# Moving a token permutation off VectorE's write side: GpSimd's sums in runs of four, ScalarE's copies with a step of 16 bytes

## The chip, the cores and the metric

One core of one Trainium2 chip. The metric is the device time of one execution in microseconds. Of the kernel before there are three timed runs and one profiled execution.

## The reference

A two-layer transformer on 2,048 tokens (2 sequences of 1,024) with 256 features. Layer 0 is causal attention with 32 query heads and 8 key/value heads of size 8, beside a gelu feed-forward in fp8. Layer 1 has an attention of a different kind, and a ternary-weight feed-forward. The change touches layer 1's attention alone. What is computed there is this:

```
def apply_rope(x, inv_freq):
    angle = t * inv_freq[None, :]
    x1, x2 = (x[..., ::2], x[..., 1::2])
    return jnp.concatenate([x1 * cos - x2 * sin, x1 * sin + x2 * cos], axis=-1)
q = (x @ wq.T).reshape(b, s, H, HD)      # H = 16 heads of HD = 16
k = (x @ wk.T).reshape(b, s, H, HD)
v = (x @ wv.T).reshape(b, s, H, HD)
q = apply_rope(q, inv_freq)
k = apply_rope(k, inv_freq)
scores = jnp.einsum('bshd,bstd->bsht', q, k) / jnp.sqrt(jnp.float32(HD))
weights = jax.nn.softmax(scores, axis=-1)
attn = jnp.einsum('bsht,bstd->bshd', weights, v)
```

So every token attends over its own 16 heads: one 16x16 table of scores for each token, none between tokens.

## The kernel before, in words

The 2,048 tokens are 16 tiles of 128. Each engine runs one fixed list of steps, written out by hand in the table ORDER (one list for TensorE, ScalarE, VectorE, GpSimd, and SyncE, which issues most DMAs). A step waits on semaphores for its inputs and for the buffers that it overwrites, so whatever stands behind a waiting step on the same engine waits too. Layer 0's attention runs through nearly all of the program in 144 "quads": four score matmuls (step qk, L761) into the four banks of psS, two exponentials of 1,024 columns on ScalarE (exp, L1057), and eight matmuls with the values (pv, L775). The score matmuls of the next quad need the banks that the exponentials of this one have read. All other work is fitted between the quads.

Layer 1's score path of tile n goes through these steps:

- **qkv1** (TensorE, L853): projected queries and keys, transposed, land in one PSUM bank as 512 columns: 2 halves (even and odd dimensions), times query and key, times 128 tokens. Three PSUM banks (psA, psB, psC) are handed round between all steps of this sort, in program order.
- **rab** (VectorE, L1512): two multiplications by cosine and sine tables from that bank into r1. A token t of the tile is a*16 + c, with a from 0 to 7 and c from 0 to 15. The output pattern puts the tokens in the order (c, a), so the 16 values that follow each other in time are written 8 floats, 32 bytes, apart. When both are done the bank is free.
- **rr** (GpSimd, L1799): a subtraction and an addition of halves of r1 into rqkv, 256 columns each, all three operands contiguous. Its outcome is 8 blocks of 32 tokens, in the order query/key, then block b = c div 4.
- **rw** and **rd** (SyncE, L563 and L571): 2 DMAs write the blocks to the DRAM scratch rscr, 4 DMAs read them back into qk1T, one for each block b: there the 16 dimensions of a head lie on the partitions, and heads and the block's 32 tokens along the columns.
- **kq** (ScalarE, L1122): two copies, queries and keys, of 512 columns from qk1T into qk1Tg (the trace calls it kTf), which bring together the tokens of one group j = c mod 4. The input pattern has runs of 8 floats. The rows of qk1T also hold an indicator pattern (ind2, read once by step mk), which masks scores between different tokens.
- **S1** (TensorE, L914): 16 matmuls from those groups into psS; then ex1 (ScalarE, L1131), PV1 (TensorE, L925), o1r and o1 (VectorE, L1552 and L1562), and a round trip through the scratch o2scr to `at`.

The pattern that reads qk1T, the products and the sums are these lines of the kernel before:

```
return qk1T[:, s, :, :].rearrange("p j n -> p (j n)").rearrange("p (h j a) -> p j h a", j=4, a=8)
...
e.tensor_tensor(r1[:, k, :].rearrange("p (e s c a) -> p e s a c", e=2, s=2, a=8), bank,
                table.unsqueeze(2).to_broadcast([128, 2, 2, 8, 16]), ALU.mult)
...
e.tensor_tensor(dst[:, 256 * f:256 * f + 256], r1[:, f, 0:256], r1[:, f, 256:512], op)
```

Of the kernel before, what the change touches and what calls it, by code (L numbers as in the profile page):

```python
# [6 lines left out]
ALU = mybir.AluOpType  # L7
ACT = mybir.ActivationFunctionType
AX = mybir.AxisListType
F32 = mybir.dt.float32  # L10
# [7 lines left out]
NT = 16  # L18
# [223 lines left out]
def shared_banks():  # L242

    fills = [s for s in first_pass("pe") + second_pass("pe") if s[0] in EMPTIED]
    return {s: k for k, s in enumerate(fills)}, fills
# [30 lines left out]
def flat(a):  # L276
    return a.rearrange("p a n -> p (a n)")


def build(nc, A):  # L280
    ctx = ExitStack()
    with ctx:
        def sb(name, shape, dt=F32):
            return ctx.enter_context(nc.sbuf_tensor(name, shape, dt))
# [4 lines left out]
        def ps(name):  # L289
            return ctx.enter_context(nc.psum_tensor(name, [128, 512], F32))  # L290

        S = {n: ctx.enter_context(nc.semaphore("s_" + n)) for n in SEMS}
# [2 lines left out]
        psV = ps("psV")  # L295
        psM = [ps("ps" + c) for c in "ABC"]
        qkvscr = nc.dram_tensor("qkvscr", [NT, 3, 128, 256], F32, kind="Internal").ap()
        rscr = nc.dram_tensor("rscr", [NT, 2, 4, 16, 512], F32, kind="Internal").ap()
        vscr = nc.dram_tensor("vscr", [NT, 16, 128, 16], F32, kind="Internal").ap()
        o2scr = nc.dram_tensor("o2scr", [NT, 16, 128, 16], F32, kind="Internal").ap()  # L300
        oscr = nc.dram_tensor("oscr", [NT, 128, 256], F32, kind="Internal").ap()
# [21 lines left out]
        turns = big[:, 1024:4096].rearrange("p (e n) -> p e n", e=3)  # L323
# [56 lines left out]
        r1 = sb("r1", [128, 2, 512])  # L380
# [3 lines left out]
        qk1T = sb("qk1T", [128, 2, 4, 128])  # L384
        G3vodd = flat(w8l[:]).bitcast(F32)[:, 512:1024].rearrange("p (g d) -> p g d", d=32)
        qk1Tg = flat(kTf[:])[:, 1280:2304].rearrange("p (s j n) -> p s j n", s=2, n=128)
# [31 lines left out]
            return (qk1Tg if n < NT else qk1T)[:, s, :, :]  # L418

        def landed(s):  # L420
            return qk1T[:, s, :, :].rearrange("p j n -> p (j n)").rearrange("p (h j a) -> p j h a", j=4, a=8)

        def of_group(n, s, b, j):

# [8 lines left out]
        def read_groups(n):  # L433

            return 64 * (n // 2 + 1) + (0 if n % 2 else 128)

        tst = [flat(r1[:]), qk1T[:].rearrange("p s j n -> p (s j n)")]
        filled, fills = shared_banks()
# [41 lines left out]
        def sp(e):  # L480
# [76 lines left out]

            def rw(n):
                src = flat(rqkv[n % 2][:, 0:2, :]).rearrange("p (f m t) -> p f m t", f=2, t=32)
                dst = rscr[n].rearrange("s b (f i) (h t) -> f (i h) (s b) t", f=2, t=32)  # L560
                for f in range(2):
                    w.wait_ge("rr", 2 * n + f + 1)
                    e.dma_start(dst[f], src[:, f, :, :]).then_inc(S[f"d_rw{n % 2}"], 16)  # L563

            def rd(n):
                w.wait_ge(f"d_rw{n % 2}", 32 * (n // 2 + 1))
                w.wait_ge("d_rd0", 128)
                w.wait_ge("kq", KQ * n)
                for b in range(4):
                    dst = qk1T[32 * b:32 * b + 16, :, :, :].rearrange("p s j n -> p s (j n)")  # L570
                    e.dma_start(dst, rscr[n, :, b].rearrange("s d n -> d s n")).then_inc(S[f"d_rd{n % 2}"], 16)  # L571

            def ow(n):
                w.wait_ge("o1", 2 * n + 2)
# [52 lines left out]
            def all_landed(passes):  # L627
# [8 lines left out]
                w.wait_ge("d_ht", 16 * NT * passes)  # L636

            run = {"first": first, "lc": lc, "lw": lw, "mk": mk, "rw": rw, "rd": rd, "wg": wg, "wt": wt, "vw": vw, "vr": vr, "ow": ow, "at1r": at1r, "out": out, "kt": kt, "qt": qt, "xt": xt, "ht": ht}
            ahead = e.mark_branch_hint_location()
            for name, n in first_pass("sp"):  # L640
# [357 lines left out]
        def act(e):  # L998
# [119 lines left out]
            def kq(n):  # L1118
                w.wait_ge(f"d_rd{n % 2}", read_groups(n))
                w.wait_ge("S1", 4 * n)  # L1120
                for s in range(2):
                    e.activation(qk1Tg[:, s, :, :].rearrange("p j (h a) -> p j h a", a=8), landed(s), ACT.Copy).then_inc(S["kq"], 1)  # L1122

            def ex1(n):
                w.wait_ge("w8", 6)
# [24 lines left out]
            def hxa(n):  # L1150
                w.wait_ge("rsg", n + 1)
                e.activation(hx_b[:, 0, :], h1, ACT.Copy, scale=ss[n % len(ss)][:, 2:3]).then_inc(S["hxa"], 1)  # L1152

            run = {"tTc": tTc, "wgx": wgx, "lx": lx, "wh": wh, "wsq": wsq, "qh": qh, "g": g, "hxa": hxa, "sin": sin, "tc": tc, "tde": tde, "exp": exp, "sq": sq, "fh": fh, "th": th, "qk1c": qk1c, "kq": kq, "gTk": gTk, "ex1": ex1,
                   "tg": tg, "ssq": ssq}
            load_small()
# [15 lines left out]
        def dve(e):  # L1172
# [328 lines left out]
                                ALU.mult).then_inc(S["v1c"], 1)  # L1501

            def rab(n):
                bank = psM[filled["qkv1", 2 * n] % len(psM)][:].rearrange("p (e s a c) -> p e s a c", e=2, s=2, a=8)
                t0 = 128 * (n % NB)
                w.wait_ge("tTc", 5)
                w.wait_ge("tc", 12)
                w.wait_ge("qkv1", 2 * n + 1)
                w.wait_ge("rr", 2 * n)
                for k in range(2):  # L1510
                    table = turns[:, k:k + 2, t0:t0 + 128].rearrange("p e (a c) -> p e a c", a=8)
                    e.tensor_tensor(r1[:, k, :].rearrange("p (e s c a) -> p e s a c", e=2, s=2, a=8), bank,  # L1512
                                    table.unsqueeze(2).to_broadcast([128, 2, 2, 8, 16]), ALU.mult).then_inc(S["rab"], 1)

            def ro1(n):
                cb = cos1[:, n % NB, :].unsqueeze(1).unsqueeze(1).to_broadcast([128, 2, 16, 8])
# [132 lines left out]
            def fl(n):  # L1649
# [7 lines left out]
                   "tw": tw, "ln0": ln0, "xn": xn, "xnTc": xnTc, "qkvc": qkvc, "va": va, "wide": wide, "q0": q0, "kl": kl, "xs": xs,  # L1657
                   "fTc": fTc, "rmax": rmax, "mTc": mTc, "ob": ob, "att": att, "attTc": attTc, "xa": xa, 
                   "ge1": ge1, "ge3": ge3, "yff": yff, "ln1": ln1, "xn1": xn1, "xn1Tc": xn1Tc, "v1c": v1c, "rab": rab, "ro1": ro1,
                   "ro2": ro2, "gTq": gTq, "m1": m1, "gTm": gTm, "o1r": o1r, "o1": o1, "sg": sg, "hh": hh,  # L1660
                   "ssm": ssm, "hx": hx, "at1Tc": at1Tc, "yo": yo, "yout": yout}
# [15 lines left out]
        def pool(e):  # L1677
# [116 lines left out]
            def rr(n):  # L1794
                dst = flat(rqkv[n % 2][:, 0:2, :])
                w.wait_ge("rab", 2 * n + 2)
                w.wait_ge(f"d_rw{n % 2}", 32 * (n // 2))
                for f, op in enumerate((ALU.subtract, ALU.add)):
                    e.tensor_tensor(dst[:, 256 * f:256 * f + 256], r1[:, f, 0:256], r1[:, f, 256:512], op).then_inc(S["rr"], 1)  # L1799

            def rsg(n):
                sn = ss[n % len(ss)]
# [2 lines left out]
                e.tensor_tensor(sn[:, 2:3], sn[:, 1:2], mhalf[:], ALU.pow).then_inc(S["rsg"], 1)  # L1805

            run = {"zero": zero, "gz": gz, "gz2": gz2, "rr": rr, "zf": zf, "w8a": w8a, "rs0": rs0, "rope": rope, "ql": ql, "mask": mask,
                   "ge4": ge4, "xf": xf, "rs1": rs1, "ro1p": ro1p, "rsg": rsg}
            ahead = e.mark_branch_hint_location()
# [35 lines left out]
def consts():  # L1845

    p = np.arange(128)
    ident = np.eye(128, dtype=np.float32)
    f = (1.0 / np.float32(10000.0) ** (np.arange(0, 8, 2, dtype=np.float32) / np.float32(8))).astype(np.float32)
    ang = (np.arange(1024, dtype=np.float32)[:, None] * f[None, :]).astype(np.float32)  # L1850
    c = np.repeat(np.cos(ang), 2, axis=1).astype(np.float32).reshape(8, 128, 8).transpose(1, 0, 2)
    s = np.repeat(np.sin(ang), 2, axis=1).astype(np.float32).reshape(8, 128, 8).transpose(1, 0, 2).copy()
    s[:, :, 0::2] *= -1
    mneg = np.where(p[None, :] > p[:, None], np.float32(NEG), np.float32(0))
    pos = (np.arange(8)[None, :] * 128 + p[:, None]).astype(np.float32)
    same = (np.arange(512)[None, :] % 8 == np.arange(8)[:, None]).astype(np.float32)
    ind2 = np.stack([NEG * same, 1.0 - same]).astype(np.float32)
    one = (p[:, None] // 16 == np.arange(8)[None, :]).astype(np.float32)
    ind1 = np.stack([NEG * one, 1.0 - one], axis=1).astype(np.float32)
    return {"ident": ident, "cs0": np.ascontiguousarray(c) * np.float32(UP), "sn0": np.ascontiguousarray(s) * np.float32(UP), "mneg": mneg, "pos": pos,  # L1860
            "ind1": ind1, "ind2": ind2}
# [35 lines left out]
```

## Time and profile before

| | us |
|---|---|
| median of 3 runs (lowest to highest) | 557.74 (557.38 to 558.65) |
| the profiled execution | 560.62 |
| span of its trace | 558.9 |
| TensorE busy in the span | 520.7 |
| ScalarE busy | 471.9 |
| VectorE busy | 381.5 |
| GpSimd busy | 233.8 |

The profiled execution took 1.7 us beside its span, and 2.9 us more than the median of the timed runs. Busy time of TensorE is modelled from its pipelined matmuls, so a short wait inside a merged group of them can be counted as busy. A row of the timeline gives start and length in us, then engine, line, operation, tiles and shape. "x2" or "x4" in it is the number of instructions merged into one row, and a bracket at the end of a row gives the idle time of the engine before it and what ended it.

### The profile page before, as it was taken

To read this page: it belongs to the slowest core of one execution; us is meant where nothing else is said; L and a number is where in the kernel's file an instruction comes from. 1 tells how busy PE (TensorE), PEld (TensorE's weight loads), DVE (VectorE), ACT (ScalarE), POOL (GpSimd) and SP (SyncE) were. 2 spreads that over 40 slices of the span, in tenths; PEclk is the share of its full clock that TensorE was granted. 3 is DMA by queue.
4 is the path that set the end of the run, shared out by engine and by line. 5 is a ranking of instruction groups with operands and counts; after the bars stand their busy time and mean duration, and the time that the engine had idled before them with its cause. 6 is when DMAs were issued, how large, how long until landed. Compare 5 with 4: busy or idle time off the path is not lost.

```text
span 558.9 us, 12847 instructions
## 1 busy us (share of the span) xinstructions
PE 520.7 (93%) x4872; PEld 261.7 (47%) x4920; DVE 381.5 (68%) x794; ACT 471.9 (84%) x614; POOL 233.8 (42%) x299
## 2 busy tenths in 40 slices
PE   7678999999999999999999999999999999998875
PEld 3323335434354555545555455564455353556544
DVE  5838887788779767766676787656554544756755
ACT  0579999999999999999989989988898998974440
POOL 3556745726534246344664565133082220160200
PEclk8869999999999999999999999999999999999988
DMA  7932112112443622345306454564533318347863
GB/s 246 326 84 58 26 41 57 41 33 39 76 82 47 103 47 59 53 66 79 67 12 122 62 83 67 93 99 67 110 56 66 64 40 142 67 83 130 112 112 88
DMA packets 211344, 46.18 MB, mean 83 GB/s; under 512 B 198544, under 2 KB 207888, under 8 KB 211280
## 3 DMA queue, kind: packets, MB, share of 16 engines
q1 hardware_dynamic: 208832, 42.37, 41.0%
q10 hardware_dynamic: 2448, 2.95, 1.7%
q8 instruction: 40, 0.66, 0.5%
q14 instruction: 24, 0.20, 0.1%
HBM read 19.09 MB, written 10.49 MB: 53 GB/s over the span
## 4 chain that ended last, share of the span: by engine, by line
PE 68%; ACT 13%; DVE 7%; DMA 5%; issue 4%; SPq 1%; POOL 1%; ACTq 0%; DVEq 0%
PE psV L775 20%; PE psS L761 8%; ACT Pt L1057 6%; PE psC L961 3%; PE psS L914 3%; PE psA L961 2%; PE psC L971 2%; PE psB L961 2%; DMA at<-o2scr 2%; DVE r L1512 2%; DMA stage<-in_wg 2%; PE psC L853 2%; PE psB L971 2%; PE psB L812 1%; PE psA L853 1%
## 5 line engine op out<-in xcount | busy, mean ns | idle before, releaser
L1057 ACT ACTIVATE Pt<-psS 128x1024 f32<-128x1024 f32 x288 | 279.9, 1031 | 27.2 <-PE psS L761 22.6
L775 PE MATMUL psV<-Pt,vaug 128*32 128x512 f32 x1152 | 150.6, 606 | 1.3 <-POOL Pt L1753 0.9
L1753 POOL TENSOR_SCALAR_AFFINE_SELECT Pt<-Pt 128x1024 f32<-128x1024 f32 x64 | 71.9, 1148 | 70.9 <-ACT Pt L1057 70.9
L761 PE MATMUL psS<-qTf,kTf 32*128 32x512 f16 x576 | 69.0, 388 | 7.7 <-DMA kTf<-QXf 4.2
L761 PEld LDWEIGHTS psS<-qTf,kTf 32*128 32x128 f16 x576 | 18.6, 91 | 92.3 <-ACT Pt L1057 47.0
L1805 POOL TENSOR_TENSOR ss<-ss,mhalf 128x1 f32<-128x1 f32 x16 | 9.3, 582 | 92.5 <-DVE ss L1589 92.5
L775 PEld LDWEIGHTS psV<-Pt,vaug 128*32 128x32 f32 x1152 | 25.0, 108 | 39.9 <-issue 31.1
L1131 ACT ACTIVATE stage<-psS 128x1024 f32<-128x1024 f32 x32 | 31.0, 1021 | 8.9 <-PE psS L914 8.8
L1799 POOL TENSOR_TENSOR rqkv<-r 128x256 f32<-128x256 f32 x32 | 24.9, 800 | 30.0 <-DVE r L1512 30.0
L1733 POOL TENSOR_TENSOR rt<-qkv,cs 128x320 f32<-128x320 f32 x16 | 15.1, 942 | 44.5 <-DVE QXf L1334 35.1
L1744 POOL TENSOR_TENSOR QXf<-rt,QXf 128x512 f16<-128x512 f32 x16 | 21.2, 1327 | 28.9 <-ACT QXf L1044 28.9
L1427 DVE SCALAR_TENSOR_TENSOR ga<-gw,gb 128x512 bf16<-128x512 f32 x32 | 23.1, 722 | 6.1 <-ACT gw L1083 6.1
L1418 DVE SCALAR_TENSOR_TENSOR gw<-gw,gb 128x512 f32<-128x512 f32 x32 | 25.1, 783 | 2.3 <-ACT gw L1072 2.2
L961 PE MATMUL psC<-wguT,xhs 128*128 128x512 bf16 x90 | 23.7, 380 | 2.4 <-issue 1.7
L1595 DVE SCALAR_TENSOR_TENSOR qtmp<-qtmp,ss 128x1024 f16<-128x1024 f32 x16 | 22.5, 1408 | 3.2 <-ACT qtmp L1152 3.2
L1152 ACT ACTIVATE qtmp<-qtmp,ss 128x1024 f16<-128x1024 f32 x16 | 18.5, 1158 | 4.5 <-POOL ss L1805 4.4
L1736 POOL TENSOR_TENSOR rt<-qkv,sn 128x160 f32<-128x160 f32 x32 | 21.9, 706 | 0.0
L1072 ACT ACTIVATE gw<-gb 128x512 f32<-128x512 bf16 x32 | 20.9, 653 | 0.0
L1083 ACT ACTIVATE gw<-gw 128x512 f32<-128x512 f32 x32 | 20.7, 646 | 0.0
L1512 DVE TENSOR_TENSOR r<-psC,big 128x512 f32<-128x512 f32 x14 | 14.5, 1120 | 8.9 <-PE psC L853 8.9
L1147 ACT ACTIVATE qtmp<-qtmp 128x1024 bf16<-128x1024 f32 x16 | 17.0, 1060 | 3.9 <-DVE qtmp L1583 2.4
L914 PE MATMUL psS<-kTf 24*128 24x128 f32 x512 | 19.5, 283 | 0.0
(339 smaller groups left out, 1088.1 us busy)
## 6 DMA issues: line engine op xcount, KB each, us to landing
rscr<-rqkv SPq DMA_DIRECT2D x32, 128.0 KB, 2.8
qk1T<-rscr SPq DMA_DIRECT2D x64, 64.0 KB, 3.0
vscr<-rqkv SPq DMA_DIRECT2D x16, 128.0 KB, 3.3
o2scr<-o SPq DMA_DIRECT2D x16, 128.0 KB, 1.7
at<-o2scr SPq DMA_DIRECT2D x16, 128.0 KB, 3.3
out<-yout SPq DMA_DIRECT2D x16, 128.0 KB, 2.7
x<-in_x ACTq DMA_DIRECT2D x3, 512.0 KB, 5.5
stage<-in_wg SPq DMA_DIRECT2D x2, 512.0 KB, 9.8
```

Of the source, the lines that this page charges most:

```text
L761: e.matmul(psS[j], kd[32 * j:32 * j + k, h, 128 * at:128 * at + 128], qd[32 * j:32 * j + k, 4 * h:4 * h + 4, :].rearrange("p s n -> p (s n ...
L775: ins = e.matmul(psV[32 * j:32 * j + 32, :], vaug[:, at, j, 32 * h:32 * h + 32], Pt[(4 * Q + j) % NP], start=(kb == 0 and h == 0), stop=(k ...
L914: ins = e.matmul(psS[b][:, 128 * j:128 * j + 128], of_group(n, 1, b, j), of_group(n, 0, b, j), start=True, stop=True)
L961: ins = e.matmul(bank[:], src[:, pt, 128 * c:128 * c + 128], wguT[:, c, c0:c0 + 512], start=(k == 0), stop=(k == 3))
L1057: e.activation(flat(Pt4[:, u % NP:u % NP + 2, :]), flat(psS4[:, j:j + 2, :]), ACT.Exp, scale=scale).then_inc(S["exp"], 1)
L1131: e.activation(P1[:, 4 * b:4 * b + 8, :].rearrange("p g n -> p (g n)"), flat(psS4[:, b:b + 2, :]), ACT.Exp, scale=SC1).then_inc(S["ex1"], 1)
L1418: e.scalar_tensor_tensor(gw[:, half, :], gw[:, half, :], 1.0 / GA, gb[:, half, :], ALU.add, ALU.mult).then_inc(S["ge1"], 1)
L1427: e.scalar_tensor_tensor(a, gw[:, half, :], 1.0, gg, ALU.add, ALU.mult).then_inc(S["ge3"], 1)
L1512: e.tensor_tensor(r1[:, k, :].rearrange("p (e s c a) -> p e s a c", e=2, s=2, a=8), bank, table.unsqueeze(2).to_broadcast([128, 2, 2, 8, 1 ...
L1595: e.scalar_tensor_tensor(hx_b[:, 1, :], h1, sn[:, 2:3], hx_b[:, 0, :], ALU.mult, ALU.subtract).then_inc(S["hx"], 1)
L1753: e.affine_select(out=p, in_=p, pattern=[[0, 8], [1, 128]], compare_op=ALU.is_ge, fill=0.0, base=0, channel_multiplier=-1).then_inc(S["mas ...
L1799: e.tensor_tensor(dst[:, 256 * f:256 * f + 256], r1[:, f, 0:256], r1[:, f, 256:512], op).then_inc(S["rr"], 1)
```

## The change

The tokens of a tile reach the scores in the same groups as before; what changes is who permutes them.

- VectorE's two products (rab) write r1 in the order in which they read, with consecutive columns.
- GpSimd's two sums (rr) read r1 in runs of four tokens, c mod 4, with 16 tokens between one run and the next, and write consecutive columns. Block b = c div 4 now stands ahead of query/key in rqkv.
- The scratch rscr has its dimensions for query/key and block exchanged. The number, the size and the rows of the DMAs rw and rd stay: 128 x 8 x 32 elements in each of 2 writes, 16 x 2 x 512 in each of 4 reads.
- ScalarE's copies (kq) read every fourth float, 16 bytes apart, in place of runs of 8; they write as before.
- The indicator ind2, a constant of the host, follows the new order of columns.

No instruction is added, removed or moved on any engine.

```
-        rscr = nc.dram_tensor("rscr", [NT, 2, 4, 16, 512], F32, kind="Internal").ap()
+        rscr = nc.dram_tensor("rscr", [NT, 4, 2, 16, 512], F32, kind="Internal").ap()
...
-            return qk1T[:, s, :, :].rearrange("p j n -> p (j n)").rearrange("p (h j a) -> p j h a", j=4, a=8)
+            return qk1T[:, s, :, :].rearrange("p j n -> p (j n)").rearrange("p (m j) -> p j m", j=4)
+
+        def by_run(a):
+            return a.rearrange("p (m b j) -> p b m j", b=4, j=4)
...
-                dst = rscr[n].rearrange("s b (f i) (h t) -> f (i h) (s b) t", f=2, t=32)
+                dst = rscr[n].rearrange("b s (f i) (h t) -> f (i h) (b s) t", f=2, t=32)
...
-                    e.dma_start(dst, rscr[n, :, b].rearrange("s d n -> d s n")).then_inc(S[f"d_rd{n % 2}"], 16)
+                    e.dma_start(dst, rscr[n, b].rearrange("s d n -> d s n")).then_inc(S[f"d_rd{n % 2}"], 16)
...
-                    e.activation(qk1Tg[:, s, :, :].rearrange("p j (h a) -> p j h a", a=8), landed(s), ACT.Copy).then_inc(S["kq"], 1)
+                    e.activation(qk1Tg[:, s, :, :], landed(s), ACT.Copy).then_inc(S["kq"], 1)
...
-                bank = psM[filled["qkv1", 2 * n] % len(psM)][:].rearrange("p (e s a c) -> p e s a c", e=2, s=2, a=8)
+                bank = psM[filled["qkv1", 2 * n] % len(psM)][:].rearrange("p (e s t) -> p e s t", e=2, s=2)
...
-                    table = turns[:, k:k + 2, t0:t0 + 128].rearrange("p e (a c) -> p e a c", a=8)
-                    e.tensor_tensor(r1[:, k, :].rearrange("p (e s c a) -> p e s a c", e=2, s=2, a=8), bank,
-                                    table.unsqueeze(2).to_broadcast([128, 2, 2, 8, 16]), ALU.mult).then_inc(S["rab"], 1)
+                    e.tensor_tensor(r1[:, k, :].rearrange("p (e s t) -> p e s t", e=2, s=2), bank,
+                                    turns[:, k:k + 2, t0:t0 + 128].unsqueeze(2).to_broadcast([128, 2, 2, 128]),
+                                    ALU.mult).then_inc(S["rab"], 1)
...
-                    e.tensor_tensor(dst[:, 256 * f:256 * f + 256], r1[:, f, 0:256], r1[:, f, 256:512], op).then_inc(S["rr"], 1)
+                    e.tensor_tensor(dst[:, 256 * f:256 * f + 256].rearrange("p (b m j) -> p b m j", b=4, j=4),
+                                    by_run(r1[:, f, 0:256]), by_run(r1[:, f, 256:512]), op).then_inc(S["rr"], 1)
...
-    same = (np.arange(512)[None, :] % 8 == np.arange(8)[:, None]).astype(np.float32)
+    same = (np.arange(512)[None, :] // 4 % 8 == np.arange(8)[:, None]).astype(np.float32)
```

## Rows read from the trace of the kernel before

**Rows 1.** Page parts 1 and 4: busy time by engine; the chain of waits by line
```profile
PE 520.7 (93%) x4872; PEld 261.7 (47%) x4920; DVE 381.5 (68%) x794; ACT 471.9 (84%) x614; POOL 233.8 (42%) x299
...
PE psV L775 20%; PE psS L761 8%; ACT Pt L1057 6%; PE psC L961 3%; PE psS L914 3%; PE psA L961 2%; PE psC L971 2%; PE psB L961 2%; DMA at<-o2scr 2%; DVE r L1512 2%; DMA stage<-in_wg 2%; PE psC L853 2%; PE psB L971 2%; PE psB L812 1%; PE psA L853 1%
```

**Rows 2.** Stages: us; PE, PEld, DVE, ACT, POOL busy; TensorE clock; DMA share, GB/s
```profile
130.00:200.00 70.00, 67.69 (x676) 33.45 (x676) 55.29 (x111) 67.37 (x91) 29.52 (x42) 1.00 0.44 75
200.00:300.00 100.00, 99.10 (x1002) 53.44 (x1006) 71.52 (x156) 94.56 (x128) 48.76 (x61) 1.00 0.35 62
300.00:400.00 100.00, 98.62 (x1020) 51.41 (x1027) 68.48 (x146) 91.11 (x118) 43.05 (x54) 1.00 0.52 82
400.00:495.00 95.00, 93.94 (x864) 43.37 (x868) 50.30 (x102) 85.66 (x105) 30.80 (x40) 1.00 0.40 71
495.00:559.00 64.00, 49.71 (x574) 34.64 (x577) 39.13 (x88) 26.12 (x37) 9.49 (x14) 0.95 0.66 110
```

**Rows 3.** VectorE's products (L1512) by bank: ns min/median/max, first and last start
```profile
L1512 DVE TENSOR_TENSOR r<-psC,big x14: 1093/1124/1152, 180.9 to 498.7; 128x512 f32<-128x512 f32 x14
L1512 DVE TENSOR_TENSOR r<-psA,big x12: 1078/1103/1159, 167.3 to 519.0; 128x512 f32<-128x512 f32 x12
```

**Rows 4.** Two VectorE operations with consecutive writes (L1574; L1399 with a broadcast input)
```profile
L1574 DVE SCALAR_TENSOR_TENSOR stmp<-stmp,psC x14: 671/687/690, 165.3 to 541.5; 128x512 f32<-128x512 f32 x14
...
L1399 DVE TENSOR_TENSOR att<-psA,rec x7: 424/424/425, 46.7 to 392.9; 128x256 f32<-128x256 f32 x7
```

**Rows 5.** Timeline of TensorE where it waited for L1512, between 130 and 495 us
```profile
140.78 0.91 PE L714 MATMUL psB<-wqkv,xnT 128*128 128x384 f32 x2 [0.58 <-DVE r L1512]
...
169.43 0.91 PE L714 MATMUL psA<-wqkv,xnT 128*128 128x384 f32 x2 [0.59 <-DVE r L1512]
...
333.27 0.81 PE L961 MATMUL psC<-wguT,xhs 128*128 128x512 bf16 x3 [0.31 <-DVE r L1512]
```

**Rows 6.** Timeline of the last two rotations: what stands around L1512
```profile
498.29 1.08 PE L925 MATMUL psB<-stage,w8l 128*32 128x128 f32 x32
499.66 0.68 DVE L1552 COPY o1r<-psB 128x512 f32<-128x512 f32 x1
...
520.16 0.83 PE L858 MATMUL psA<-wqkv,xhs 128*128 128x256 f16 x6 [0.68 <-DVE r L1512]
520.92 1.17 PE L914 MATMUL psS<-kTf 24*128 24x128 f32 x32
```

**Rows 7.** ScalarE's copies (L1122) and other SBUF-sourced ScalarE operations, by source line
```profile
L1122 ACT ACTIVATE kTf<-qk1T x32: 613/637/696, 153.4 to 535.7; 128x512 f32<-128x512 f32 x32
...
L1083 ACT ACTIVATE gw<-gw x32: 629/641/690, 32.3 to 479.3; 128x512 f32<-128x512 f32 x32
...
L1147 ACT ACTIVATE qtmp<-qtmp x16: 1057/1058/1070, 150.5 to 543.8; 128x1024 bf16<-128x1024 f32 x16
```

**Rows 8.** Timeline after the first pair of copies: ScalarE, then TensorE
```profile
153.40 1.15 ACT L1122 ACTIVATE kTf<-qk1T 128x512 f32<-128x512 f32 x2
...
160.52 1.94 ACT L1057 ACTIVATE Pt<-psS 128x1024 f32<-128x1024 f32 x2
...
160.06 0.39 PE L761 MATMUL psS<-qTf,kTf 32*128 32x512 f16 x4
...
162.22 0.68 PE L761 MATMUL psS<-qTf,kTf 32*128 32x512 f16 x4
```

**Rows 9.** Timeline: the third pair and TensorE after it; ScalarE after the twelfth
```profile
193.92 1.19 ACT L1122 ACTIVATE kTf<-qk1T 128x512 f32<-128x512 f32 x2
...
197.22 0.39 PE L761 MATMUL psS<-qTf,kTf 32*128 32x512 f16 x2 [0.18 <-ACT Pt L1057]
...
485.60 1.94 ACT L1057 ACTIVATE Pt<-psS 128x1024 f32<-128x1024 f32 x2 [1.00 <-PE psS L761]
```

**Rows 10.** GpSimd's sums (L1799), and a product in rows of four (L1736)
```profile
L1799 POOL TENSOR_TENSOR rqkv<-r x32: 722/731/1708, 135.4 to 520.9; 128x256 f32<-128x256 f32 x32
...
L1736 POOL TENSOR_TENSOR rt<-qkv,sn x32: 587/602/1587, 12.8 to 413.4; 128x160 f32<-128x160 f32 x32
```

## The prediction

> **What bounds the kernel now.** I read the page first, then the busy time by stage, then the three lines that the change touches, and last the timeline around them. The page says TensorE: it is busy for 93% of the span, and the chain of waits consists mostly of its matmuls [rows 1]. The stage table shows that a share over the whole span hides how close ScalarE is [rows 2]. Over the 365 us from 130 to 495, TensorE is busy for 67.69 + 99.10 + 98.62 + 93.94 = 359.4 us, which leaves 5.6 us idle, and ScalarE for 67.37 + 94.56 + 91.11 + 85.66 = 338.7 us, which leaves 26.3. VectorE is busy for 245.6 us of it and GpSimd for 152.1, so neither is short of time; their delays matter only where somebody waits. TensorE's granted clock is full there. From 495 on all engines have gaps, and the path runs through transfers and short steps.
>
> Between TensorE and ScalarE the coupling is tight: four score matmuls need banks that two exponentials must have read. When nothing holds them, four take 0.39 us; at 162.22 they took 0.68, since the second two could start only when the exponentials of the row at 160.52, ending at 162.46, were through [rows 8]. So "busy" contains short waits for ScalarE that no idle column shows. Most of what follows hangs on this.
>
> **VectorE's products get shorter.** There are 32 of them (2 in each of 16 tiles), and they take about 1.11 us [rows 3]. The nearest operation with the same 512 columns, PSUM as one input, SBUF as another and fp32 out, but consecutive writes, takes 0.687 [rows 4]. I take that: 1.11 - 0.69 = 0.42 us less for each, 0.84 for a pair, 13.5 us of VectorE time in all. The other end is no saving (if the broadcast table, which stays, is what costs); another product with a broadcast input, 256 columns in 0.424, speaks against that [rows 4]. Little of the 13.5 is on the path. The chain gives L1512 2% of the span, some 11 us [rows 1], but TensorE had other matmuls to run during most of it; what it can win is its idle time. Between 130 and 495 us it waited for these products at three places, 0.58, 0.59 and 0.31 us, each under what the products become shorter: 1.5 us [rows 5]. Of the last two tiles, the pair before the copy at 499.66 sits on the path, but that copy also needs the matmuls of 498.29, which end at 499.37, so 0.3 at most. At 520.16 TensorE waited 0.68, but the scores of tile 14 at 520.92 wait for ScalarE's copies, not for VectorE, so most of that turns into a longer wait there; I count 0.2 [rows 6]. Sum: **2.0 us gained**, with 1 and 3 as ends.
>
> **ScalarE's copies read with a step of 16 bytes.** 32 copies of 0.637 us each now read runs of 8 floats, and cost the same as a contiguous activation with SBUF input, 0.641 [rows 7]. So runs of 32 bytes cost nothing. No row shows ScalarE reading single elements far apart. Lower end: no cost. Upper end: the nearest row for single elements at a large step is VectorE's write with 32 bytes between elements, which costs 0.42 more for 512 elements than the consecutive one [rows 3, 4]. For ScalarE, 512 more elements cost 1.058 - 0.641 = 0.417 us, so one lost slot for each element comes to the same 0.42 [rows 7]. If each element took VectorE's whole 1.11 / 512 = 2.17 ns, a copy would take 1.11, or 0.47 more. I take 0.42, since VectorE's row is the only one here with one element per place fetched, and its extra is just that of one slot per element: a copy of **1.06 us**, a pair 0.84 us later.
>
> What 0.84 us costs at the end depends on ScalarE's next gap. I followed ScalarE from each of the 12 pairs before 495 us until either its gaps made up 0.84 us or a score matmul started as its exponential ended. The first pair, at 153.40, finds no gap before the contact at 162.22, so TensorE loses nearly all of it [rows 8]. The third, at 193.92, meets TensorE already waiting for it at 197.22. The twelfth has a gap of 1.00 before the row at 485.60, and only a contact ahead of that gap costs something [rows 9]. By this reading four pairs (tiles 0, 2, 3, 9) cost about 0.8 each, four (1, 6, 7, 8) about 0.55, two (4, 11) about 0.3 and two (5, 10) nothing: 3.2 + 2.2 + 0.6 = 6.0. Behind 495 the copies of tile 14 delay the scores at 520.92 [rows 6], 0.6 more. TensorE's 5.6 us of idle take back perhaps 1. Sum: **5.6 us lost**, with 0 and 8 as ends.
>
> Here a rule speaks against the change. The row: VectorE's writes with a single float per 32 bytes take 1.11 us where consecutive ones take 0.69 [rows 3, 4]. The Trainium skill, "SBUF — State Buffer", in the note on cachelines under "Door 1: The DMA port swizzle", says that SBUF has lines of 16 bytes and that full bandwidth needs two or more accesses to a line. A step of 16 bytes is one access to a line, so by that rule the copies slow down; by the row of the contiguous activation alone they would not, and the sum would be -2.0.
>
> **GpSimd's sums read in runs of four.** Two a tile, 0.731 us now [rows 10]. The nearest row with short runs is the rotation product of layer 0, 160 elements with a step of 8 bytes in rows of four: 0.602, or 3.8 ns an element. At that rate 256 take 0.96; the lower end is 0.73. I take 0.8, nearer to the contiguous end, since the elements inside a run stay neighbours. At the upper end a pair is 0.46 later, less than the 0.84 by which the products end sooner. The two DMAs behind it, the masks and the power steps queued behind it on GpSimd (busy for 152 of 365 us [rows 2]) are covered by that and by the time to the copies: the first sum starts at 135.4 and the first copy at 153.4, 18 us later [rows 7, 10]. Cost: 0. Without that cover it would be 16 x 0.14 = 2 us. Product, sum and copy are queued where they were, SyncE's DMAs keep number and size, so the exchanged dimensions of rscr cost 0: the transfer is hidden in the same 18 us.
>
> **The sum.** -2.0 + 5.6 + 0 = +3.6. Against the profiled execution, 560.6 us beside a span of 558.9, that is 564.2; that execution was 2.9 above the median of the timed runs, 557.74, which I forecast from: 557.7 + 3.6 = 561.3. My sum for ScalarE has more ways to come out smaller than larger (a contact moved past a gap costs nothing), so I round down to **560.9**.
>
> **The rivals.**
> *ScalarE doesn't mind the step.* Then only the products' gain is left: 557.7 - 2.0 = 555.7, with 554.5 to 556.8. For it: 32-byte runs are free, and ScalarE's 0.82 ns per element (0.417 / 512) leaves memory more slack than one element per VectorE slot may. Against: VectorE's row. It decides at 2.0 / 5.6 x 0.42 = 0.15: a copy that becomes longer by less than 0.15 us makes the change a gain. The same note of the Trainium skill also says that four fp32 is as far as one can stride for free, which speaks for this case; no row here shows a step of exactly 16 bytes.
> *The products don't get shorter*, since the broadcast table or the two tables in one instruction cost the time: 0 gained, 5.6 lost, 563.3; without ScalarE's cost 557.7, no change, so the change wouldn't do what it says. Against: the product with a broadcast input and consecutive writes, whose 0.424 us for 256 columns fits 0.687 for 512 [rows 4].
> *GpSimd becomes slow.* If each run of four is handled as a row of its own and a sum takes 1.5 us, a pair is 1.5 later, 0.7 more than the products give back; masks and the reciprocal roots behind it come late in some tiles, and I put 8 x 0.3 = 2.4 us on it: 558.1 with free copies. The Trainium skill, "GPSIMD Engine Reference", section "Performance pitfalls for Q7 kernels", says that reads with a step above 8 bytes cost half as much again; inside a run of four the step is 4 bytes, and at half as much again (1.1 us) the pair would be covered.
>
> **How the numbers follow.** Three runs of the kernel before spread over 1.3 us, so I take 0.2%, 1.1 us, as what a measurement can tell from no change. The forecast case has 0.56: within it slower 0.46, same 0.08, faster 0.02. The free step has 0.36: faster 0.27, same 0.08, slower 0.01. Unchanged products have 0.05: slower 0.03, same 0.02. Slow GpSimd has 0.03, 0.01 each. Sum: faster 0.30, same 0.19, slower 0.51. The likeliest case's own range is 558.5 to 563.8. The range over all cases goes from 554.6, near the low end of the free step, to 563.8; a tenth is left out on either side.
>
> **What the changed profile would show.** The products near 690 ns. The copies near 1,060 ns (forecast) or 640 (first rival), and that row settles the sign. The sums at 730 to 960 ns. ScalarE's busy time up by 32 x 0.42 = 13 us, VectorE's down by as much. TensorE's waits for L1512 gone between 130 and 495, and more or longer waits of the score matmuls for L1057. I am wrong if the copies stay at 640, or if they double and the time stays: then ScalarE's gaps had taken the delay in.

## The result and the profile after

| | before | changed |
|---|---|---|
| median of 4 runs, us | 557.98 (557.38 to 558.65) | 570.78 (568.65 to 574.83) |
| the profiled execution, us | 560.62 | 568.65 |
| span of its trace, us | 558.9 | 566.9 |

The ratio is 1.0242, with a 95% interval from 1.0202 to 1.0281: 13 us slower. The forecast had the sign right and the likeliest case right, but said 3.2 us and a range that ended at 563.8. In a second comparison with more runs, told below, the same kernel came to 1.0178 (1.0147 to 1.0208), 10 us. Both lie outside the range.

The three lines of the change, by source line (ns min/median/max, first and last start), in the changed kernel. They answer to [rows 3], [rows 7] and [rows 10]:

```profile
L1514 DVE TENSOR_TENSOR r<-psC,big x14: 678/685/693, 179.0 to 505.6; 128x512 f32<-128x512 f32 x14
...
L1125 ACT ACTIVATE kTf<-qk1T x32: 1113/1144/1255, 151.4 to 545.9; 128x512 f32<-128x512 f32 x32
...
L1802 POOL TENSOR_TENSOR rqkv<-r x32: 714/724/1803, 133.4 to 527.0; 128x256 f32<-128x256 f32 x32
```

The products are at 0.685 us, as taken. GpSimd's sums in runs of four cost what contiguous ones cost, 0.724. The copies went from 0.637 to 1.144, 0.51 us more each, 16 us for the 32. The page's busy line, and the stages (us; PE, PEld, DVE, ACT, POOL busy; clock; DMA share, GB/s), against [rows 1, 2]:

```profile
PE 527.7 (93%) x4920; PEld 262.9 (46%) x4920; DVE 370.6 (65%) x794; ACT 487.6 (86%) x614; POOL 232.0 (41%) x299
```

```profile
130.00:200.00 70.00, 68.32 (x671) 33.67 (x668) 50.80 (x108) 69.02 (x90) 30.41 (x42) 1.00 0.44 75
200.00:300.00 100.00, 98.63 (x997) 52.27 (x994) 68.74 (x152) 94.58 (x125) 47.70 (x59) 1.00 0.32 58
300.00:400.00 100.00, 98.04 (x1006) 52.26 (x1006) 64.81 (x145) 92.72 (x115) 41.76 (x54) 1.00 0.48 76
400.00:495.00 95.00, 93.73 (x852) 42.29 (x848) 46.53 (x101) 87.18 (x102) 26.41 (x35) 1.00 0.43 78
```

ScalarE's busy time grew by 15.7 us. VectorE's fell by 10.9, less than the 13 that the prediction named: the products' own busy time fell by 12.5, and other lines of VectorE differ between the two traces by up to 0.9 either way. TensorE's share hardly moved: it is still "busy" for 358.7 of the 365 us. Whoever looks at busy shares alone sees a kernel bound by TensorE in both, and no reason for 8 us more span. The waits tell more. Here are TensorE's between 130 and 495 us in the changed kernel (engine, line waited for: us in total, times, longest); before, the first two lines of this list were 0 and 0.2 us, and L1512 stood in it with 1.5:

```profile
PE psS L917 <- ACT Pt L1060: 2.4, 8, 0.3
PE psS L764 <- ACT Pt L1060: 2.4, 5, 0.5
PE psC L856 <- ACT gb L1068: 0.6, 1, 0.6
PE psC L815 <- DVE stmp L1577: 0.5, 1, 0.5
```

The waits for the products are gone. The new first line is one that the prediction had not looked at: L917 (L914 before) is S1, the scores of layer 1 themselves, and it waits for the *exponentials* of layer 0, eight times.

### The profile page after: what moved, and what is told of

It reads as the page before. It is cut to its first block, busy times and chain, and to the rows that moved or that the text cites. A ratio compares the mean times of both kernels' runs of the same rounds, so it can differ in the third digit from the quotient of the medians.

```text
span 566.9 us, 12895 instructions
## 1 busy us (share of the span) xinstructions
PE 527.7 (93%) x4920; PEld 262.9 (46%) x4920; DVE 370.6 (65%) x794; ACT 487.6 (86%) x614; POOL 232.0 (41%) x299
## 4 chain that ended last, share of the span: by engine, by line
PE 58%; ACT 24%; issue 7%; DVE 4%; DMA 3%; SPq 2%; POOL 1%; ACTq 0%; DVEq 0%; POOLq 0%
PE psV L778 17%; ACT Pt L1060 13%; PE psS L764 7%; ACT kTf L1125 4%; PE psS L917 3%; PE psC L964 3%; PE psA L964 2%; DMA stage<-in_wg 2%; PE psB L964 2%; PE psC L856 2%; PE psB L974 1%; DMA kTf<-QXf 1%; PE psB L815 1%; PE psA L815 1%; POOL Pt L1756 1%
## 5 line engine op out<-in xcount | busy, mean ns | idle before, releaser
L1125 ACT ACTIVATE kTf<-qk1T 128x512 f32<-128x512 f32 x32 | 35.2, 1162 | 0.3 <-DMA qk1T<-rscr 0.3
L1736 POOL TENSOR_TENSOR rt<-qkv,cs 128x320 f32<-128x320 f32 x16 | 16.0, 1003 | 45.4 <-DVE QXf L1337 35.8
L1747 POOL TENSOR_TENSOR QXf<-rt,QXf 128x512 f16<-128x512 f32 x16 | 19.9, 1245 | 29.6 <-ACT QXf L1047 29.6
L917 PE MATMUL psS<-kTf 24*128 24x128 f32 x512 | 23.2, 295 | 6.0 <-ACT kTf L1125 3.5
L964 PE MATMUL psC<-wguT,xhs 128*128 128x512 bf16 x104 | 27.7, 390 | 0.0
L917 PEld LDWEIGHTS psS<-kTf 24*128 24x128 f32 x512 | 18.9, 194 | 12.3 <-ACT kTf L1125 4.9
L964 PE MATMUL psB<-wguT,xhs 128*128 128x512 bf16 x80 | 20.6, 380 | 0.0
```

Of the source, the lines that this page charges most:

```text
L917: ins = e.matmul(psS[b][:, 128 * j:128 * j + 128], of_group(n, 1, b, j), of_group(n, 0, b, j), start=True, stop=True)
L964: ins = e.matmul(bank[:], src[:, pt, 128 * c:128 * c + 128], wguT[:, c, c0:c0 + 512], start=(k == 0), stop=(k == 3))
L1125: e.activation(qk1Tg[:, s, :, :], landed(s), ACT.Copy).then_inc(S["kq"], 1)
```

## The experiments

Eleven runs were made; the ninth is the changed kernel once more. All ratios are against the kernel before on the same chip.

**1. GpSimd does the whole permutation.**

```
# products as changed (consecutive columns); copies, rw, rd, rscr, ind2 as before; in rr:
-  e.tensor_tensor(dst[:, 256*f:256*f+256], r1[:, f, 0:256], r1[:, f, 256:512], op)
+  e.tensor_tensor(dst[:, 256*f:256*f+256].rearrange("p (s c a) -> p s c a", s=2, a=8),
+                  by_token(r1[:, f, 0:256]), by_token(r1[:, f, 256:512]), op)
# by_token(a) = a.rearrange("p (s a c) -> p s c a", s=2, a=8)
```

> VectorE's consecutive writes kept; GpSimd's sums do the whole permutation (reads with a step of 64 bytes), so ScalarE's copies and the DMAs stay as in the kernel before. Theory A (all of the loss is ScalarE's longer copies): copies back at 0.64 us, products at 0.69, time 1 to 3 us below the kernel before (555 to 557), whatever the sums take as long as that is under 1.6 us. Theory B (the loss comes from the changed order of r1 or from the products' earlier end, not from ScalarE): still 5 us or more above the kernel before. If GpSimd pays for each single element, its sums go from 0.73 to 1.1 or more.

Measured: 0.9966 (0.9934 to 0.9999), 1.9 us faster. The sums rose to 1.098 us, the copies were back at 0.637:

```profile
L1802 POOL TENSOR_TENSOR rqkv<-r x32: 1061/1098/2177, 136.2 to 519.8; 128x256 f32<-128x256 f32 x32
...
L1125 ACT ACTIVATE kTf<-qk1T x32: 612/637/698, 154.3 to 534.7; 128x512 f32<-128x512 f32 x32
```

Theory A holds: with short copies the shorter products are a small gain, the size forecast (2.0), and GpSimd's 0.37 us more a sum is covered. It is also the only version with the right groups that came out ahead of both kernels, if by little: its interval ends at 0.9999.

**2. One more copy a tile**, no strided read:

```
 for s in range(2):
+    if s == 0:
+        w.wait_ge("more", n)
+        e.activation(more, landed(s), ACT.Copy).then_inc(S["more"], 1)   # 512 columns, read by nobody
     e.activation(qk1Tg[:, s, :, :]..., landed(s), ACT.Copy).then_inc(S["kq"], 1)
```

> The kernel before plus one more ScalarE copy of 512 columns a tile, with the old pattern, into columns that nobody reads: 16 x some 0.52 us of ScalarE time, 8.3 us, and no strided read. Theory A (a delay of ScalarE goes through nearly in full): 6 to 8.5 us slower, 564 to 566. Theory C (my forecast's share, 5.6 of 13.4, and something else behind the rest): 3.5 us slower, 561 to 562.

Measured: 1.0077 (1.0038 to 1.0115), 4.3 us for 7.5 us more of ScalarE's busy time. Nearer to theory C; with an interval from 2.1 to 6.4 us theory A's lower end is not excluded.

**3. The copies in quarters**, the same pattern and data:

```
-    e.activation(qk1Tg[:, s, :, :]..., landed(s), ACT.Copy).then_inc(S["kq"], 1)
+    for j in range(4):
+        ins = e.activation(qk1Tg[:, s, j, :]..., landed(s)[:, j, :, :], ACT.Copy)
+    ins.then_inc(S["kq"], 1)
```

> The kernel before with each of the 32 copies cut into 4 copies of 128 columns, the same pattern and data: ScalarE pays fixed costs only, some 0.3 to 0.5 us more per 512 columns. Whatever a tile's copies take more by the trace, d: theory A says the time grows by 0.8 to 1.0 x 16 x d; theory C says 0.42 x 16 x d.

Measured: 1.0086 (1.0052 to 1.012), 4.8 us for 7.7 us of busy time. A share of 0.6 again, between the two theories, and the interval of 2.9 to 6.7 us excludes neither. A plain, unstrided delay of ScalarE costs time; whether it explains 15 us was open.

**4. The cost of a step, by itself.** The kernel before, and behind its last step:

```
+ src = stepped(big[:, 1024:4096], k)      # 384 fp32 elements, k elements apart; or dst in Pt
+ ScalarE: e.activation(dst, src, ACT.Copy)
+ VectorE, GpSimd: e.tensor_tensor(dst, src, src, ALU.mult)
```

> The kernel before with measurements behind its last step: 384 fp32 elements read from SBUF with a step of 1, 2, 3, 4, 5 and 8 elements, then written with a step of 2, 4 and 8, two of each on ScalarE, VectorE (product of a tensor with itself) and GpSimd. If lines of 16 bytes need two accesses each, steps of 1 and 2 cost the same and 4, 5, 8 more, 3 between. For ScalarE a step of 4 should then add about 0.37 us (0.5 x 384 / 512). If the cost grows with distance, 8 costs more than 4. Its total time means nothing.

The timeline of ScalarE: reads with a step of 1, 2, 3, 4, 5 and 8 elements, then writes with a step of 2 and 4:

```profile
555.66 0.52 ACT L500 ACTIVATE Pt<-big 128x384 f32<-128x384 f32 x1 [9.71 <-DVE flag L1685]
...
557.34 0.54 ACT L500 ACTIVATE Pt<-big 128x384 f32<-128x384 f32 x1
557.92 0.71 ACT L500 ACTIVATE Pt<-big 128x384 f32<-128x384 f32 x1
559.40 0.88 ACT L500 ACTIVATE Pt<-big 128x384 f32<-128x384 f32 x1
561.22 0.88 ACT L500 ACTIVATE Pt<-big 128x384 f32<-128x384 f32 x1
563.05 0.89 ACT L500 ACTIVATE Pt<-big 128x384 f32<-128x384 f32 x1
...
565.46 0.54 ACT L500 ACTIVATE Pt<-big 128x384 f32<-128x384 f32 x1
566.04 0.88 ACT L500 ACTIVATE Pt<-big 128x384 f32<-128x384 f32 x1
```

VectorE, reads with a step of 1, 3 and 4; then GpSimd, reads with a step of 1 and 8:

```profile
570.29 0.56 DVE L502 TENSOR_TENSOR Pt<-big 128x384 f32<-128x384 f32 x1
...
572.06 0.66 DVE L502 TENSOR_TENSOR Pt<-big 128x384 f32<-128x384 f32 x1
573.46 0.83 DVE L502 TENSOR_TENSOR Pt<-big 128x384 f32<-128x384 f32 x1
...
583.53 0.83 POOL L502 TENSOR_TENSOR Pt<-big 128x384 f32<-128x384 f32 x1 [38.76 <-DVE Pt L502]
...
589.03 0.88 POOL L502 TENSOR_TENSOR Pt<-big 128x384 f32<-128x384 f32 x1
```

On ScalarE and VectorE a step of 8 bytes costs next to nothing (0.54 and 0.56 us against 0.52 and 0.56), and 16 bytes the whole penalty (0.88 and 0.83); beyond 16 next to nothing is added. A step of 12 bytes costs half of the penalty on ScalarE (0.71) and over a third on VectorE (0.66). Writes behave as reads. The Trainium skill, "SBUF — State Buffer", in the note on cachelines under "Door 1: The DMA port swizzle", says that a line has 16 bytes and wants at least two accesses for full bandwidth. The trace agrees: on ScalarE 0.54 at a step of 2 elements, 0.88 at 4. The same note says that four fp32 is as far as one can stride for free. There the trace differs: step 4 is at 0.88, and the measurement decides. GpSimd loses 0.05 us of 0.83 in this form.

**5. The step alone**, in the kernel before. The groups of the scores then hold other tokens than they should:

```
-  landed: .rearrange("p (h j a) -> p j h a", j=4, a=8)
+  landed: .rearrange("p (m j) -> p j m", j=4)
```

> The kernel before with one pattern changed: ScalarE's copies read every fourth column. The groups of the scores then hold other tokens than they should; every instruction, DMA and size is that of before. Theory A (the copies' 0.5 us each is all of the loss): the changed kernel's loss plus what the first experiment gained, 12.8 + 1.9 = 14.7, so 570 to 574. Theory C (the delay costs 0.5 to 0.6 of itself, as in the two dose runs, and the rest of the loss comes from GpSimd's reads, rscr or the products): 16.2 x 0.55 = 9, so 566 to 568.

Measured: 1.0212 (1.0162 to 1.0262), 11.8 us slower: this one pattern costs about as much as the whole change. The loss lies between the theories' 14.7 and 9 us, with an interval (9.1 to 14.6) that reaches close to both; the next run decides.

**6. The changed kernel with copies of consecutive columns.** Here too the groups hold other tokens:

```
-  e.activation(qk1Tg[:, s, :, :], landed(s), ACT.Copy)
+  e.activation(qk1Tg[:, s, :, :], qk1T[:, s, :, :], ACT.Copy)
```

> The changed kernel with ScalarE's copies reading 512 consecutive columns; the groups of the scores then hold other tokens than they should, all else is as changed. Theory A: as the first experiment, 1 to 3 us under the kernel before. Theory C: 3 to 5 us over it.

Measured: 0.9952 (0.9922 to 0.9983), 2.7 us *faster* than before. Theory C falls: with the changed products, sums, scratch layout and DMAs in place, nothing of the loss is left once the copies are short (their median is 0.635 us here).

**7. Both doses at once** (2 and 3 together):

> The kernel before with both doses at once: one more copy of 512 columns a tile, and all copies cut in four; no strided read. ScalarE's extra time by the single doses is 7.5 + 7.7 = 15.2 us, nearly the changed kernel's 15.7 to 16.2. If a delay's cost grows in proportion (single doses: 4.3 and 4.8 us), it takes 9 us more, 567 to 568. If the first 0.5 us of a tile's delay finds slack that the second no longer finds, 12 to 15 us more, 570 to 574, and theory A holds with a cost that bends upwards.

Measured: 1.0200 (1.0154 to 1.0245), 11.2 us for 16.3 us more of ScalarE's busy time, beside 11.8 for 15.9 in run 5. Two plain kinds of delay cost what the step costs, so the step acts through time alone. The traces say it more sharply. From the first pair of copies to the twelfth, ScalarE takes 328.2 us before (153.40 to 481.58), 337.7 in run 5 and 337.8 here. Single doses sum to 9.1 us in the timed runs, less than the 11.2 of both, but within the noise. In the same stretch of the traces they add 3.9 and 4.1 us singly and 9.7 together, so the cost does bend upwards, though less than I had put.

**8. The copies on VectorE**, on top of run 1:

```
 ORDER["act"]: the 16 kq steps taken out;  ORDER["dve"]: put in at the places that correspond in time
-  e.activation(qk1Tg..., landed(s), ACT.Copy)
+  e.tensor_copy(qk1Tg..., landed(s))
```

> The first experiment's kernel (VectorE writes consecutive columns, GpSimd permutes all) with the copies of runs of 8 moved from ScalarE to VectorE, in VectorE's order at the places that correspond in time to ScalarE's in the first experiment. ScalarE's list loses 18.6 us of work, VectorE's gains 32 x about 0.6. Theory A, turned round (a tile's ScalarE time that goes away comes back at the end by half or more, until TensorE alone binds): 3 to 8 us under the first experiment, 548 to 553. If TensorE is the bound and ScalarE only when it is made slower: within 1.5 us of the first experiment, 554 to 557.

A miss: 1.0033 (1.0004 to 1.0062), 1.8 us slower than before and 3.7 slower than run 1, though ScalarE's busy time fell from 471.7 to 456.4 us. Most copies took 0.42 us there, some 1.3:

```profile
L1425 DVE COPY kTf<-qk1T x32: 404/420/1306, 151.1 to 536.7; 128x512 f32<-128x512 f32 x32
```

Time taken off ScalarE did not come back at the end. Between 130 and 495 us ScalarE now waits longer for TensorE's score matmuls, first in run 1, then here:

```profile
ACT Pt L1060 <- PE psS L764: 16.8, 36, 1.2
...
ACT Pt L936 <- PE psS L640: 25.2, 50, 1.2
```

So what mostly passes on when it is added gave nothing when it was taken away. The run is no pure subtraction: VectorE took the copies on, and in that stretch TensorE waits 1.8 us for VectorE, where run 1 has no such wait. What the shorter ScalarE list would give alone is not shown.

**9. The changed kernel once more**, five runs:

> The changed kernel once more, beside the next two and in more rounds, since its runs spread over 1.1%. By the traces the loss between 130 and 495 us adds up (9.5 for the copies, 1.7 back for the products), so I expect 2.12% less 0.34 to 0.48%, that is 1.65 to 1.8%, or 567 to 569 against 558; if it is 2.4% again, some 3 us more come from something that neither single change has.

Measured: 1.0178 (1.0147 to 1.0208), within the expected 1.65 to 1.8%. Copies (+2.12) and products (-0.34) add up; no third cost is needed. The first four runs had 1.0242, and the two intervals overlap by little. The two profiled executions, 566.9 and 570.2 us long, show where such spread comes from. From the first pair of copies to the twelfth they take 337.0 and 336.9 us. The 3.3 us between them lie ahead of 130 us (1.1 us, at a granted clock of 0.97 and 0.93) and behind the start of the last two exponentials (2.2 us, at 0.94 and 0.90).

**10 and 11. Values before scores.** In TensorE's order, `S1.n pv.m` became `pv.m S1.n` at eight tiles, in the changed kernel and in run 1's.

> The changed kernel with one more edit: in TensorE's order the scores S1 of tiles 0, 1, 4, 5, 7, 8, 9 and 10 go behind the quad's values matmuls (pv) that now follow them. S1 needs banks that two exponentials queued behind the long copies must have read; pv needs only older exponentials. Theory S (the contact that passes the copies' delay on is S1, not the next quad's score matmuls): TensorE no longer idles ahead of L917 for L1060 (8 places before, 2 to 4 now) and wins some 0.5 to 0.8 us at each of 6 to 8 tiles: 3 to 6 us under the changed kernel. Theory Q (the delay passes on at the next quad's score matmuls whatever S1 does), and also if ScalarE's ex1, which now comes later, costs what TensorE wins: within 1.5 us of the changed kernel, or slower.

> The first experiment's kernel with the same eight exchanges. With short copies S1 starts as its banks come free, so there is little idle time to win: theory S says 0 to 1.5 us under the first experiment (554 to 556), or up to 2 over it where ex1 comes later. If it wins as much as the run above, the exchange helps by itself and says nothing about the copies.

Measured: 1.0243 (1.0208 to 1.0277) and 1.0091 (1.006 to 1.0121). Both expectations missed. By the ratios both are slower than without the exchange, by 3.6 us (against run 9; the changed kernel's first four runs had 1.0242, no less than here) and 7.0. The exchange moved the wait instead of removing it: ScalarE's ex1 comes later, and now the next quad's score matmuls (L640 in this numbering) wait for *it*, in run 11:

```profile
PE psS L640 <- ACT stage L1010: 4.9, 13, 0.5
PE psS L640 <- ACT Pt L936: 0.2, 1, 0.2
```

Run 10 has the same first row with 4.8 us. ScalarE's own idle time ahead of ex1 grew as well, between 130 and 495 us from 1.9 (run 9) to 6.7 us in run 10, and from 2.8 (run 1) to 10.6 in run 11.

With the exchange the long copies cost 2.43 - 0.91 = 1.5%, without it 1.78 + 0.34 = 2.1%. The difference of 0.6% has an uncertainty of as much (four ratios, each known to 0.3 to 0.35%), and the longer gaps ahead of ex1 could take in a part of the delay by themselves. So these two runs don't show how much of the copies' cost runs through S1's place. The choice of tiles was not right for it either. In the changed kernel's trace S1 waits for an exponential at tiles 0, 1, 4, 6, 7 and 10. Tile 6, whose S1 already stood behind values matmuls, was left as it was; tiles 5, 8 and 9, where S1 does not wait, were exchanged. And "pv needs only older exponentials" did not hold everywhere: at tile 7 of run 10 the values matmuls waited 1.1 us for one.

## Why the prediction was right in kind and wrong in size

**The products: right.** 0.42 us less each, forecast 2.0 us in all; run 1 gave 1.9, run 6 2.7. The three waits of [rows 5] vanished.

**GpSimd, DMAs, scratch layout: right.** Sums 0.724 where 0.8 was taken. Run 6 holds all of these changes and loses nothing.

**A copy's length: taken 1.06, measured 1.144.** The step at fault is "its extra is just that of one slot per element". Run 4 shows that the extra does not carry over from VectorE to ScalarE. An element 16 bytes from the next costs ScalarE its 0.82 ns plus (0.88 - 0.52) / 384 = 0.94, so 1.76 ns; it costs VectorE its 1.03 ns (0.687 less 0.424 for 256 columns [rows 4]) plus (0.83 - 0.56) / 384 = 0.70, so 1.73. The *absolute* time per element is common to both engines, the extra is not. The fixed part of a copy, 0.637 - 512 x 0.82 / 1000 = 0.22, plus 512 x 1.76 gives 1.12. The prediction had this length among its ends (2.17 ns an element, VectorE's fixed part included, 1.11 us) and chose the other.

**What a late ScalarE costs: taken 5.6 us, measured 11.8 (run 5).** This is the step that failed. Three things are in it: the copy's length (0.51 in place of 0.42), the contacts that were summed to 6.0 us, and "TensorE's 5.6 us of idle take back perhaps 1". A contact is a place where TensorE starts at the moment at which an exponential ends, so that a later exponential makes TensorE later.

The contacts first. I followed ScalarE from each pair of copies to the next *score matmul of layer 0* or until gaps had made up the delay. The trace of before shows what I passed over. Tile 4, ScalarE, then TensorE:

```profile
260.73 1.16 ACT L1122 ACTIVATE kTf<-qk1T 128x512 f32<-128x512 f32 x2
261.77 1.95 ACT L1057 ACTIVATE Pt<-psS 128x1024 f32<-128x1024 f32 x2
...
264.95 1.94 ACT L1131 ACTIVATE stage<-psS 128x1024 f32<-128x1024 f32 x2 [0.23 <-PE psS L914]
```

```profile
263.65 1.27 PE L914 MATMUL psS<-kTf 24*128 24x128 f32 x32
264.86 1.07 PE L775 MATMUL psV<-Pt,vaug 128*32 128x512 f32 x8
```

And the same place in the changed kernel:

```profile
261.73 2.16 ACT L1125 ACTIVATE kTf<-qk1T 128x512 f32<-128x512 f32 x2
263.76 1.95 ACT L1060 ACTIVATE Pt<-psS 128x1024 f32<-128x1024 f32 x2
...
266.87 1.94 ACT L1134 ACTIVATE stage<-psS 128x1024 f32<-128x1024 f32 x2
```

```profile
264.94 0.49 PE L917 MATMUL psS<-kTf 24*128 24x128 f32 x4 [0.22 <-ACT Pt L1060]
265.76 1.16 PE L917 MATMUL psS<-kTf 24*128 24x128 f32 x28 [0.33 <-ACT Pt L1060]
266.85 1.07 PE L778 MATMUL psV<-Pt,vaug 128*32 128x512 f32 x8
```

S1 writes the same four score banks as the quads, so it too must wait for the exponentials queued right behind the copies. Before, these ended at 263.72, and S1, which had started at 263.65 with the first two banks, went on at once. Changed, they end at 265.71 and the rest of S1 starts at 265.76. The pair of copies starts 1.00 later than before (261.73 and 260.73) and what follows S1 starts 1.99 later (266.85 and 264.86), so the whole second took effect. Before, nobody idled there, and so no row of the wait list named it. By my way of counting, ScalarE's gap of 0.23 ahead of ex1 was slack, too. It is none: ex1 waits for S1, S1 for the exponentials behind the copies, so the gap stands *behind* the contact in the chain, and moves with it.

The same for all tiles. The middle row is how much further behind the kernel before run 5 falls between one pair of copies and the next (first 154.23 - 153.40 = 0.83, then 182.97 - 181.28 = 1.69, so 0.86; for tile 11, to the last exponential); the last row the same for run 2, whose delay is half:

| tile | 0 | 1 | 2 | 3 | 4 | 5 | 6 | 7 | 8 | 9 | 10 | 11 | sum |
|---|---|---|---|---|---|---|---|---|---|---|---|---|---|
| forecast, for a delay of 0.84 | 0.8 | 0.55 | 0.8 | 0.8 | 0.3 | 0 | 0.55 | 0.55 | 0.55 | 0.8 | 0 | 0.3 | 6.0 |
| run 5, delay about 1.03 | 0.86 | 0.92 | 0.87 | 1.06 | 1.01 | 0.40 | 0.87 | 1.02 | 0.85 | 1.06 | 0.58 | 0.52 | 10.0 |
| run 2, delay about 0.52 | 0.37 | 0.40 | 0.28 | 0.49 | 0.53 | 0.00 | 0.39 | 0.51 | 0.31 | 0.52 | 0.06 | 0.02 | 3.9 |

Scaled to 1.03 the forecast would be 7.4: of the missing 4, size is 1.4 and contacts 2.6. The tiles with S1 shortly behind the copies and a low forecast (1, 4, 6, 7) make up 1.4 of those, and tile 10, where the forecast had nothing and S1 now waits as well, 0.6. At tile 5 (0.4) the trace names no wait at S1. That the delay goes through S1 at these tiles is read from the traces; no run isolates it. The rows also explain why a double dose costs over twice: a tile passes on its delay less a fixed slack of 0 to 0.5 us. Tiles 5, 10 and 11 keep back half a microsecond and pass on nothing of a single dose. The changed kernel shows the same increments (1.00 for tile 4, 0.39 for tile 5), but for 0.67 less at tile 0, where the wait at 169.43 of [rows 5] had been. In run 1 the pairs of copies gain 0.66 at tile 0 and another 0.33 at tile 5, behind the wait at 333.27; in the changed kernel that second gain does not show.

Then the idle time. That idle time takes "back perhaps 1" had no row behind it. TensorE's idle was waits for VectorE and short issue gaps, and these move along with TensorE when it is late; in run 5 nothing came back. The timed runs' 11.8 us less 10.0 leave 1.8 for what lies behind the last exponential, where I had 0.6, but the interval on 11.8 is 2.8 wide on either side, and the profiled executions don't show it: from the start of the last two exponentials to the end they take 65.8 us before (493.10 to 558.9) and 65.0 in run 5 (503.95 to 568.9).

**The rivals.** The free step was the case on the other side, and run 4 excludes it. Its threshold of 0.15 stays open: by run 2, a copy longer by 0.26 on average costs 4.3 us (2.1 to 6.4), more than twice the gain, which in proportion puts the break-even at 0.12, and higher if the slack of tiles 5, 10 and 11 takes the first part. Unchanged products and slow GpSimd did not happen.

**The test I had named.** "The copies near 1,060" with the time between 558.5 and 563.8; the row came, the time did not follow, and the reason is in what I did not list as a possible contact.

What stays open: how much of the cost at S1 could be had back with another order. The exchange tried made run 1's kernel slower and the changed one no faster. The tail behind 495 us was not taken apart.

## What to carry to other kernels

When an engine that is busy for 93% of a stage gets a longer instruction, assume that the delay passes on in full, and take off only slack that a row shows, tile by tile. In runs 2, 3, 5 and 7, 0.57 to 0.74 of ScalarE's added time reached the end. To find the places, list everyone who writes a buffer that the delayed engine reads, not only the consumer you have in mind; places with zero slack and no idle time appear in no wait list until they are late. An engine's gap is slack only if what ended it does not itself depend on the delayed work.

A permutation cost least where runs stayed together: runs of 8 floats on ScalarE (0.637 us, consecutive 0.641) and runs of 4 on GpSimd (0.724, consecutive 0.731) were free. Otherwise it cost least on an engine off the path: run 1 put it, at 0.37 us a sum, on GpSimd, for which neither TensorE nor ScalarE waited between 130 and 495 us.

## What the hardware showed that I had not expected

On ScalarE and VectorE an fp32 element 16 bytes from the next takes some 1.75 ns (by the working above), whichever the engine's own rate (0.82 and 1.03 ns an element). Steps of 20 and 32 bytes take the same to 0.02 us for 384 elements, and so do writes with steps of 16 and 32 (0.88 and 0.89 us on ScalarE, 0.83 and 0.85 on VectorE). GpSimd reads single elements 32 bytes apart at 0.88 us for 384, against 0.83 consecutive, but its sums with a step of 64 bytes and rows of eight took 1.098 against 0.731. And the schedule repeats itself closely: the delays that tiles passed on agreed within some 0.05 us between the changed kernel, its repetition and run 5 at all tiles but the first, where the products' gain sits, while whole executions of one kernel spread over 1%.
